# One adaLN block, batch by batch: where in SBUF the two operands of a matmul stand to each other

## The reference

```python
ga = (2 * (ga >= 0) - 1) * jnp.maximum(jnp.abs(ga), 0.25)      # gb in the same way
h = _layernorm(x, axis=-1) * (1 + ca) + sa
x = x + ga * attn(h)      # scores = (h * w_lhs) @ (h * w_rhs).T; softmax(scores, axis=2) @ h
h = _layernorm(x, axis=-1) * (1 + cb) + sb
x = x + gb * ffn(h)       # relu(h @ W1 + b1) @ W2 + b2, 256 -> 1024 -> 256
```

## Time and profile before

| | before |
|---|---|
| median of 3 runs | 675.46 us (674.22 to 675.6) |
| span of the profiled execution | 672.1 us |
| what lies around the span, by the median | 3.4 us |
| PE busy | 665.8 us (99%), 4481 matmul records |
| DVE busy | 549.5 us (82%) |
| ACT busy | 513.4 us (76%) |
| POOL busy | 299.3 us (45%) |
| mean granted clock of PE | 1.000 |

### The profile page before, as it was taken

The page is one execution under the profiler, slowest core; times in us unless marked ns, Lnnn a source line. Parts: engine busy times, 40 slices in busy tenths (PEclk is TensorE's granted clock), DMA queues, the critical chain, the costliest instruction groups (busy, mean ns, idle before and its releaser), DMA issues.

```text
span 672.1 us, 13438 instructions
## 1 busy us (share of the span) xinstructions
PE 665.8 (99%) x4481; PEld 612.9 (91%) x4481; DVE 549.5 (82%) x1139; ACT 513.4 (76%) x763; POOL 299.3 (45%) x311
## 2 busy tenths in 40 slices
PE   8999999999999999999999999999999999999998
PEld 8688898998999999999999989999899999999997
DVE  4799879998899789997899898998899977787321
ACT  2367779994899769995899948998599976677463
POOL 3471365155543364523547245352554333625444
PEclk9999999999999999999999999999999999999999
DMA  8141665237732578135662267513773246401300
GB/s 293 55 87 63 196 181 181 80 126 241 184 109 95 137 237 234 47 118 157 189 207 78 94 220 212 130 62 128 254 203 70 96 158 178 140 17 65 101 33 32
DMA packets 76929, 92.27 MB, mean 137 GB/s; under 512 B 9120, under 2 KB 67040, under 8 KB 76896
## 3 DMA queue, kind: packets, MB, share of 16 engines
q1 hardware_dynamic: 76896, 91.85, 45.4%
HBM read 55.33 MB, written 36.50 MB: 137 GB/s over the span
## 4 chain that ended last, share of the span: by engine, by line
PE 97%; DVE 2%; DMA 1%; issue 0%; SPq 0%; ACT 0%; DVEq 0%; ACTq 0%
PE col L675 9%; PE col L674 9%; PE col L673 9%; PE acc L595 8%; PE score L775 8%; PE acc L596 8%; PE acc L601 8%; PE score L771 8%; PE score L772 8%; PE score L663 4%; PE score L662 4%; PE score L664 4%; PE score L764 4%; PE score L636 2%; DMA S<-wmod 1%; PE score L751 1%
## 5 line engine op out<-in xcount | busy, mean ns | idle before, releaser
L1264 POOL TENSOR_TENSOR hid_lo<-hid,hid_hi 128x512 fp32r<-128x512 f32 x127 | 177.6, 1407 | 202.1 <-ACT hid_hi L800 201.7
L796 ACT ACTIVATE hid<-col,b1T 128x512 f32<-128x512 f32 x128 | 87.0, 679 | 69.9 <-PE col L675 65.2
L595 PE MATMUL acc<-W2hi,hid_hi 128*128 128x256 f32 x480 | 117.1, 278 | 0.0
L596 PE MATMUL acc<-W2lo,hid_hi 128*128 128x256 f32 x480 | 116.7, 278 | 0.0
L771 PE MATMUL score<-V,Phi 128*128 128x258 f32 x448 | 108.7, 281 | 0.0
L772 PE MATMUL score<-V,Phi 128*128 128x256 f32 x448 | 108.5, 281 | 0.0
L675 PE MATMUL col<-h2hi,W1lo 128*128 128x512 f32 x256 | 100.9, 394 | 0.0
L674 PE MATMUL col<-h2lo,W1hi 128*128 128x512 f32 x256 | 100.6, 393 | 0.0
L673 PE MATMUL col<-h2hi,W1hi 128*128 128x512 f32 x256 | 100.4, 392 | 0.0
L800 ACT ACTIVATE hid_hi<-hid 128x512 fp32r<-128x512 f32 x128 | 81.0, 633 | 15.3 <-PE acc L601 11.1
L595 PEld LDWEIGHTS acc<-W2hi,hid_hi 128*128 128x128 f32 x480 | 90.3, 188 | 2.5
(11 more groups left out here) (168 smaller groups left out, 1470.5 us busy)
## 6 DMA issues: line engine op xcount, KB each, us to landing
block_rows<-blocks SPq DMA_DIRECT2D x29, 512.0 KB, 2.6
blocks<-block_rows SPq DMA_DIRECT2D x116, 128.0 KB, 2.9
x_cur<-x SPq DMA_DIRECT2D x16, 512.0 KB, 4.1
ln_t<-x SPq DMA_DIRECT2D x14, 512.0 KB, 4.6
score_blocks<-stage SPq DMA_DIRECT2D x14, 512.0 KB, 3.0
S<-score_blocks SPq DMA_DIRECT2D x56, 128.0 KB, 3.6
S<-quarter_blocks SPq DMA_DIRECT2D x56, 96.0 KB, 2.3
out<-x_mlp SPq DMA_DIRECT2D x8, 512.0 KB, 3.6
```

Of the source, the lines that this page charges most:

```text
L595: nc.tensor.matmul(o, hi, W2hi[:, it, :], start=(it == 0 and (apart or t % 2 == 0)), stop=False, skip_group_check=True)
L596: nc.tensor.matmul(o, hi, W2lo[:, it, :], start=False, stop=False, skip_group_check=True)
L796: nc.scalar.activation(hid[:, n % 2, :], col[n % 2][:], ACT.Relu, bias=b1T[:, n % FT:n % FT + 1]).then_inc(col_read, 1)
L1264: G.tensor_tensor(hid_lo[:, n % RING, :], hid[:, n % 2, :], hid_hi[:, n % RING, :].bitcast(F32), ALU.subtract).then_inc(hid_lo_done, 1)
```

## The change: addresses, pitches and a row of matmuls at the end

The operands are placed anew. What matters to the text is the address of the moving operand less that of the stationary one, modulo 512 bytes, for the two operands of the same matmul. It follows from the order and the sizes of the declared tensors:

| kind | stationary, moving before | distance before | stationary, moving after | distance after |
|---|---|---|---|---|
| second layer | 192, 128 | -64 | 192, 128 | -64 |
| first layer | 128, 192 | +64 | 128, 64 | -64 |
| scores | 64, 64 | 0 | 320, 256 | -64 |
| values, 256 or 258 columns of key tile t | 64, 64 + 32t or 80 + 32t | 32t or 16 + 32t | 192 + 16t, 128 + 16t | -64 |

`V` had rows of 2 x 260 elements (2080 bytes) with its second half 260 elements in; now its rows have 516 elements (2064 bytes), the second half 256 elements in, and the ones stand behind the second half alone. `Phi`, `Plo` and `soft` were `[3 slots, 8 tiles, 128]` in one piece; now they are 8 rows, one for each key tile, of 3 x 128 + 4 elements (1552 bytes), and a slot is 128 elements of each row. Small tensors and named gaps fill the room between, so that the addresses come out as in the table. `stage`, `stage_lr` and the quarter that is staged in `soft` overlap other slots than before, so the first of the eight `Phi` copies now waits for the two stage stores that the second and third copies waited for.

```diff
-    VP = D + 4
+    VP, VROW = D, 2 * D + 4
+    RROW = RING * P + 4
...
+        sb("before_Phi", [P, 32])
+        by_slot = lambda rows: rows[:, :, 0:RING * P].rearrange("p t (s c) -> p s t c", c=P)
...
-        Phi, Plo = sb("Phi", [P, RING, T, P], F32R), sb("Plo", [P, RING, T, P], F32R)
+        Phi = by_slot(sb("Phi_rows", [P, T, RROW], F32R)[:])
+        sb("behind_Phi", [P, 96])
+        Plo = by_slot(sb("Plo_rows", [P, T, RROW], F32R)[:])
...
+        sb("before_R", [P, 40])
         Rhi, Rlo = sb("Rhi", [P, DK, ROWS], F32R), sb("Rlo", [P, DK, ROWS], F32R)
...
-        V = sb("V", [P, T, 2 * VP], F32R)
+        V = sb("V", [P, T, VROW], F32R)
...
+        sb("before_h2", [P, 64])
         h2hi, h2lo = sb("h2hi", [P, DK, ROWS], F32R), sb("h2lo", [P, DK, ROWS], F32R)
...
                             last.then_inc(tile_done, 1)
+                        for w_at, h_at, count in ((0, 32, 5), (0, 24, 4), (0, 20, 4), (16, 0, 5),):
+                            for _ in range(count):
+                                nc.tensor.matmul(col[0][:, 0:512], W1hi[:, 0, w_at:w_at + P], h2hi[:, 0, h_at:h_at + 512], start=True, stop=True)
...
                         for t in range(T):
-                            nc.tensor.matmul(o, Phi[:, slot, t, :], V[:, t, 0:VW], start=(t == 0), stop=False)
-                            nc.tensor.matmul(o[:, 0:D], Phi[:, slot, t, :], V[:, t, VP:VP + D], start=False, stop=False)
+                            nc.tensor.matmul(o, Phi[:, slot, t, :], V[:, t, VP:VP + VW], start=(t == 0), stop=False)
+                            nc.tensor.matmul(o[:, 0:D], Phi[:, slot, t, :], V[:, t, 0:D], start=False, stop=False)
...
-                        if n == 1:
+                        if n == 0:
                             act.wait_ge(stage_stored[1], 16 * b)
-                        elif n == 2:
-
                             act.wait_ge(quarter_stored[1], 16 * b)
...
-                        for half in range(2):
-                            V_.memset(V[:, :, half * VP + D:half * VP + D + 1].bitcast(F32), 1.0)
-                            V_.memset(V[:, :, half * VP + D + 1:half * VP + VW].bitcast(F32), 0.0)
+                        V_.memset(V[:, :, VP + D:VP + D + 1].bitcast(F32), 1.0)
+                        V_.memset(V[:, :, VP + D + 1:VP + VW].bitcast(F32), 0.0)
```

More of the change, by code:

```diff
@@ L282, in block_kernel @@
             pass
-        with nc.sbuf_tensor("stage", [P, 2, Q, HT, 2, QP], F32) as stage, \
-                nc.sbuf_tensor("stage_lr", [P, T, P], F32) as stage_lr, nc.sbuf_tensor("soft", [P, RING, T, P], F32) as soft:
-            stage_q = [q.rearrange("p a b -> p (a b)")[:, 0:Q * TURNS * QP] for q in (soft[:, RING - 1], stage_lr[:])]
-        Phi, Plo = sb("Phi", [P, RING, T, P], F32R), sb("Plo", [P, RING, T, P], F32R)
+        sb("before_Phi", [P, 32])
+        by_slot = lambda rows: rows[:, :, 0:RING * P].rearrange("p t (s c) -> p s t c", c=P)
+        with nc.sbuf_tensor("stage", [P, 2, Q, HT, 2, QP], F32) as stage, nc.sbuf_tensor("stage_lr", [P, T, P], F32) as stage_lr, \
+                nc.sbuf_tensor("behind_stage", [P, 128], F32), nc.sbuf_tensor("soft_rows", [P, T, RROW], F32) as soft_rows:
+            soft = by_slot(soft_rows[:])
+            stage_q = [q[:].rearrange("p a b -> p (a b)")[:, 0:Q * TURNS * QP] for q in (soft_rows, stage_lr)]
+        Phi = by_slot(sb("Phi_rows", [P, T, RROW], F32R)[:])
+        sb("behind_Phi", [P, 96])
+        Plo = by_slot(sb("Plo_rows", [P, T, RROW], F32R)[:])
         with nc.sbuf_tensor("L_first", [P, DK, ROWS], F32) as L_first, nc.sbuf_tensor("R_first", [P, DK, ROWS], F32) as R_first:
@@ L292, in block_kernel @@
         Lhi, Llo = sb("Lhi", [P, DK, ROWS], F32R), sb("Llo", [P, DK, ROWS], F32R)
+        mod_l, mod_r, w_sign, w_abs = sb("mod_l", [P, 2 * DK]), sb("mod_r", [P, 2 * DK]), sb("w_sign", [P, 2, DK]), sb("w_abs", [P, 2, DK])
+        w_root, root_power = sb("w_root", [P, 2, DK]), sb("root_power", [P, 2, DK])
+        root, root_r, sign_r = sb("root", [P, DK]), sb("root_r", [P, DK]), sb("sign_r", [P, DK])
+        sb("before_R", [P, 40])
         Rhi, Rlo = sb("Rhi", [P, DK, ROWS], F32R), sb("Rlo", [P, DK, ROWS], F32R)
-        with nc.sbuf_tensor("V_unsplit", [P, T, 2 * VP], F32) as V_unsplit:
+        row_max, part_max = sb("row_max", [P, T]), sb("part_max", [P, 2, 4, HT])
+        nm1, rs1, nb1, nb2 = sb("nm1", [P, T]), sb("rs1", [P, T]), sb("nb1", [P, T]), sb("nb2", [P, T])
+        inv_sum = sb("inv_sum", [P, 1])
+        sb("before_V", [P, 16])
+        with nc.sbuf_tensor("V_unsplit", [P, T, VROW], F32) as V_unsplit:
             V_first = V_unsplit[:, :, VP:VP + VW]
-        V = sb("V", [P, T, 2 * VP], F32R)
-        sb("behind_V", [P, 96])
+        V = sb("V", [P, T, VROW], F32R)
+        stats1, mv1, mv2, half_power = sb("stats1", [P, HT, 6]), sb("mv1", [P, T, 2]), sb("mv2", [P, T, 2]), sb("half_power", [P, HT])
+        nm2, rs2 = sb("nm2", [P, T]), sb("rs2", [P, T])
+        sb("behind_V", [P, 32])
         x_cur = sb("x_cur", [P, T, D])
@@ L310, in block_kernel @@
         hid_hi, hid_lo = sb("hid_hi", [P, RING, HR], F32R), sb("hid_lo", [P, RING, HR], F32R)
+        stats, var_eps = sb("stats", [P, HT, 6]), sb("var_eps", [P, HT])
+        sb("before_h2", [P, 64])
         h2hi, h2lo = sb("h2hi", [P, DK, ROWS], F32R), sb("h2lo", [P, DK, ROWS], F32R)
[L312 to L322, removed]
         wmod_a = S[:, 7, :].rearrange("p (k n) -> p k n", k=DK)
```

## The result

| | before | after |
|---|---|---|
| median | 675.17 us (674.22 to 675.6, 4 runs) | 677.59 us (677.28 to 678.09, 4 runs) |
| ratio | | 1.0041, 95% interval 1.003 to 1.0053 |
| span of the profiled execution | 672.1 us | 675.5 us |

The account below looks back on a forecast made before the run. Bound: the tensor engine, matmul count times distance between starts. Gains 6.7 + 3.7 + 6.8 + 2.0 = 19.2 us, less 2.4 given back and 0.9 tail, leave 15.9: span 656.2, plus 3.4 around it, 659.6 us; range 652 to 669.

Parts of the forecast that it names:

- The table of losses by own distance: All four matmul kinds: losses sort by operand distance, 6.6 ns for second layer at -64, 13.3 for 256-column scores at 0.
- Item 1: Values matmuls: reach the second layer's loss, 113.8 ns, gaining 6.7 us over 1344 matmuls; ends 0 and 12.2 us.
- values-left-out rival: Values gain nothing, with stationary rows off a multiple of 64 bytes and the next tile's 80 off; 665.4 us, 12%.
- Item 2: Scores matmuls of 256, 384 and 512 columns: gains of 1.1, 1.3 and 1.3 us, sum 3.7 us.
- Item 3: First layer, 512 columns: down to 222.0 ns, gaining 6.8 us over 768 matmuls; ends 3.3 and 11.5 us.
- Item 4: Second layer, own distance unchanged: in-step predecessors gain 1.3 ns over 1512 matmuls, 2.0 us; ends 0 and 3.2.
- Item 5: The 18 matmuls at the program's end, in nobody's results: run past the last store, adding 0.9 us (0.6 to 1.2).
- Items 6 and 7: ACT's and DVE's pitched rows cost 0, ends -1 and +1 us; first Phi copy's wait for two stage stores costs 0.
- Given back: Values' start with Plo: faster tensor engine waits there for the other engines, giving back 2.4 us; ends 1 and 4.
- addresses don't matter: Rival for all matmuls: losses belong to the kinds, not addresses; 676.4 us with the tail, 5%.
- The slower rival: Values: stationary rows off a multiple of 64 bytes cost more than distance gives back, 126 ns; 679.8 us, 5%.
- The skill's rule: All matmuls: two independent SBUF read ports, weight loading takes no bandwidth, so the addresses are worth nothing.

Follow-up runs that it names:

- a1: Matmuls alone on one core, 24 per address pair, no kernel computation; 512 columns took 227.1 ns at distance 0, 229.6 at +64, 233.3 at -64.
- b1: Matmuls alone, 24 per entry, distances in steps of 16 at 256 and 258 columns; values' order before took 119.1 ns, as changed 119.5.
- c1: Matmuls alone in steps of 6, 12 and 24 like the kernel's, pitches of 16 bytes; values 118.9 ns in the order before, 119.2 as changed.
- d1: Matmuls alone in the loop's 6, 12, 6, 12, 24 sequence, twice, with true row pitches; values 119.2 ns as changed, 118.6 at distance 16.
- a4_v_alone: Changed kernel without the 18 end matmuls, first layer and scores back at old distances, so only the values at -64; ratio 1.0025 to the kernel before.
- a3_h2_alone: Kernel before with only h2hi and h2lo moved, first layer's distance from +64 to -64; ratio 1.0005 to the kernel before.
- e2_values_16: Changed kernel's row pitches with values at constant distance 16, first layer and scores as before, no 18 end matmuls; ratio 0.9998 to the kernel before.
- b2_h2_zero: Kernel before with only h2hi and h2lo moved to 128, first layer's distance from +64 to 0; ratio 1.0005 to the kernel before.

## Why the prediction was wrong, by its steps

- *The matmuls' distance is the time, and address sets part of it*: right. Runs a1, b1, c1 and d1 show it with nothing else running. But address sets it only together with what ran before.
- *The table of losses by own distance*: this is the step that failed. It read the second layer's small loss (6.6 ns) as the effect of -64, from one width, and carried it to three others. The runs show that -64 is good at 256 columns only (272 cycles at best, 282.6 in its other rate), bad at 512 (560 against 549 where the first layer stood) and nothing special at 258 (290) or for the pair of 258 and 256 (283). Two extra columns were enough: the values' 258 were taken for the second layer's 256. The step also named evidence against itself and didn't use it: first-layer steps at one address took 233.3 and 228.3 ns, a spread of 5.0, nearly the 6.7 between the scores and the second layer that the table explained.
- *Item 1, values*, 6.7 us gained: 1.1 lost (a4_v_alone: +0.79 ns). The values-left-out rival gave them nothing; the lower end of the range should have been below nothing, since no row had a constant distance at 258 columns.
- *Item 2, scores*, 3.7 gained: 0.2 gained in all, 256 columns -2.4 ns (forecast -6.7, so the inference fell short even at its own width), 512 columns +1.9 (forecast -8.0), 384 columns -0.4 (forecast -7.7).
- *Item 3, first layer*, 6.8 gained: 1.3 lost (a3_h2_alone: +1.8 ns). Its lower end, 3.3, supposed that the sign of the effect was known.
- *Item 4, second layer*, 2.0 gained: 0.7 lost, though its neighbour effect is real. Behind the new first layer it does go from about 115.2 to 114.3 ns; behind the new values it goes from 114.7 to 118.2.
- *Item 5, tail*: +0.9 forecast, about 1.0 in the span by its rows; in the runs' medians it doesn't stand out. Its starts gave the rates at 512 columns: 228.6 ns at +64, 229.8 at +32, 233.5 at +16, 232.5 at -128. In a1_distances +32 was worse than +16 (233.3 and 231.7), so in groups of 4 or 5 the distance alone doesn't set the loss, which is what the prediction wanted to learn from them.
- *Items 6 and 7, pitched rows and the moved wait*: 0 forecast, 0 measured. *Given back*, 2.4 us of new Plo waits: none came, because nothing got faster.
- *The rivals*: "addresses don't matter" came nearest in time (676.4) but its reason was wrong, so that was luck. The slower rival had the right place, the values, and the wrong mechanism: rows off a multiple of 64 bytes are harmless (e2_values_16). Slower deserved far more than 5%, since every gain hung on one inference that no row tested.
- *The skill's rule*: The Trainium skill, "TensorE: Matmul & The Clock Gate", section "Step-by-step: what each phase is for", says that loading the next weights takes nothing from the running matmul's reads. Run a1_distances differs from it: the place of the stationary operand alone moves 512 columns from 544 to 560 cycles. The size is what counts here, though. In steps as short as the kernel's, the sequences with a values tile in runs c1 and d1 lie within 1.2% of each other (16.72 to 16.91 us for two rounds of 60 matmuls), so the rule's forecast was the better one for this kernel.

Open: how the place of the stationary operand comes to cost time (that its loading meets the moving reads is a guess: every matmul of these runs loads its weights anew, and no run took the two reads apart), and what picks the fast or the slow rate when a step begins. The span of one profiled execution grew by 3.4 us; by the ratio of the runs the change costs 2.8 us (2.0 to 3.6), tail included.

## What to carry to other kernels

A correlation over four kinds of work that differ in width, order and neighbours is not a measurement of one of these traits: before a layout is built on it, time each width alone at each distance, and then in steps as long as the kernel's. Of the gains of a settled rate, steps of 6 to 24 matmuls kept half or less (2.2 ns alone, 1.1 in b2_h2_zero; 6.7 forecast and 2.4 measured for the scores of 256 columns), and the neighbour step can lose as much, so a change is worth what the whole sequence gives and not what its own step shows.

## What the runs showed of the hardware

- Alone on the core, float32r matmuls back to back take 272 to 289 cycles of 2.4 GHz for 256 columns and 544 to 568 for 512, by the moving operand's address less the stationary one's (a1_distances, b1_distances_fine); moving both changes nothing. Modulo 256 bytes holds at 512 columns for 0, 64, 128 and 192; -16 took 568 in one run and 560 in the other.
- The order of good distances differs by width: 192 and 112 for 256 columns (272), 0 for 512 (544), 16 for 258 (279.8 against 286 to 293).
- At the same addresses there are two rates, and what ran before picks one: 256 columns at -64 ran at 113.3 to 115.5 ns or at 117.8 to 118.4, and the 512 columns next to them at 229.0 or 232.2 (d1_real_pitches, and the kernels before and after). The bank of PSUM doesn't pick it.
